# Two expert phases of a one-core macaron kernel: a wait inside the scatters, another order for the first statistics, and tables built in five parts

## What is computed

```python
x = x + 0.5 * ffn(layernorm(x)); x = x + mamba(layernorm(x)); x = x + 0.5 * ffn(layernorm(x))
def ffn(x):                       # x: 2048 tokens of 512
    logits = x @ router_w.T       # 8 experts, the 2 best of each token
    scores, top_idx = top_k(logits, 2)
    y_e = (silu(x @ wg[e]) * (x @ wu[e])) @ wd[e]          # e: 8 experts, inner width 256
    shared = silu(x @ sg_w + sg_b) * (x @ su_w + su_b) @ sd_w + sd_b
    return sum_over_best(scores * y_e) + shared
```

## Time and profile before

| | |
|---|---|
| median of 3 runs | 2316.42 us (2307.47 to 2318.51) |
| profiled execution | 2313.75 us, span 2312.0 us, mean granted TensorE clock 0.967 |
| PE, DVE, ACT, POOL busy | 93%, 64%, 62%, 60% of the span |
| `ffn1`, `ffn2` in the span | 0 to some 360 us, 1953.7 to 2312 us |

### The profile page before, as it was taken

One profiled execution on the slowest core, in us unless ns is written; L12 is line 12 of the kernel. 1 busy time (PEld: TensorE's weight loads), 2 busy tenths in 40 slices (PEclk: granted clock), 3 DMA queues, 4 the chain that ended last, 5 costly groups with the idle time before them and its releaser, 6 DMA issues. The chain is left out here.

```text
span 2312.0 us, 42896 instructions
## 1 busy us (share of the span) xinstructions
PE 2156.3 (93%) x11718; PEld 1744.5 (75%) x11718; DVE 1474.8 (64%) x2947; ACT 1432.8 (62%) x2960; POOL 1376.3 (60%) x1242
## 2 busy tenths in 40 slices
PE   5899996899999999999988999999999997789996
PEld 3687774688888888888767888888888885577775
DVE  6532247577777677777887777777777778732225
ACT  5133323777787778787658787778777774423331
POOL 2886351476666667666517666667666663586622
PEclk8999997899999999999999999999999998899998
DMA  9665361334334333433214434334433431555545
GB/s 345 243 189 175 115 174 42 101 111 108 106 84 119 106 101 99 119 97 93 65 49 127 110 86 126 98 98 105 113 102 88 117 85 35 186 188 164 160 142 164
DMA packets 204904, 285.32 MB, mean 123 GB/s; under 512 B 16288, under 2 KB 148458, under 8 KB 204816
## 3 DMA queue, kind: packets, MB, share of 16 engines
q1 hardware_dynamic: 185936, 219.18, 33.1%
q0 software_dynamic: 18880, 65.02, 9.3%
HBM read 225.43 MB, written 58.72 MB: 123 GB/s over the span
## 5 line engine op out<-in xcount | busy, mean ns | idle before, releaser
L2057 PE MATMUL mamba_p_proj<-mamba_xt_lo,mamba_in_hi 128*128 128x512 f32 x1056 | 456.9, 433 | 1.6 <-DVE mamba_bc L1708 1.1
L1708 DVE SCALAR_TENSOR_TENSOR mamba_xs<-mamba_p_proj,mamba_taps,mamba_xs 128x511 f32<-128x511 f32 (+2 forms) x384 | 285.8, 744 | 258.9 <-ACT mamba_xs L1455 250.0
L2059 PE MATMUL mamba_p_proj<-mamba_xt_hi,mamba_in_lo 128*128 128x512 f32 x1056 | 416.2, 394 | 0.0
L2058 PE MATMUL mamba_p_proj<-mamba_xt_hi,mamba_in_hi 128*128 128x512 f32 x1056 | 414.0, 392 | 0.0
L1328 POOL TENSOR_TENSOR mamba_xend<-mamba_xdt,mamba_to_end_g 128x512 f32<-128x512 f32 x128 | 134.0, 1047 | 340.0 <-DVE mamba_xdt L1768 282.8
L1334 POOL TENSOR_TENSOR mamba_mix<-mamba_mix,mamba_scores 128x512 f32<-128x512 f32 x256 | 326.5, 1297 | 14.2 <-ACT mamba_mix L1521 14.2
L1517 ACT ACTIVATE mamba_mix<-mamba_cum_l,mamba_cum_g 128x128 f32<-128x128 f32 x1024 | 324.7, 388 | 8.7 <-DMA mamba_cum_l<-mamba_cum_rows 3.8
L664 DVE TENSOR_TENSOR ffn_h<-ffn_p_gu,ffn_sil 128x256 f32<-128x256 f32 x110 | 46.8, 426 | 317.9 <-ACT ffn_sil L546 303.9
L546 ACT ACTIVATE ffn_sil<-ffn_p_gu 128x256 f32<-128x256 f32 x110 | 42.3, 385 | 319.4 <-PE ffn_p_gu L913 237.5
L2059 PEld LDWEIGHTS mamba_p_proj<-mamba_xt_hi,mamba_in_lo 128*128 128x128 f32 x1056 | 199.6, 189 | 46.5
L2057 PEld LDWEIGHTS mamba_p_proj<-mamba_xt_lo,mamba_in_hi 128*128 128x128 f32 x1056 | 200.7, 190 | 40.7 <-DVE mamba_bc L1708 2.0
(11 more groups left out here) (344 smaller groups left out, 5095.0 us busy)
## 6 DMA issues: line engine op xcount, KB each, us to landing
mamba_cum_l<-mamba_cum_rows SPq DMA_DIRECT2D x128, 512.0 KB, 5.3
mamba_rise<-mamba_exp_rows SPq DMA_DIRECT2D x256, 128.0 KB, 3.4
ffn_xs<-slots_in SPq DMA_DIRECT2D x78, 256.0 KB, 2.7
slots_out<-ffn_y SPq DMA_DIRECT2D x78, 256.0 KB
mamba_raw_x<-in_t SPq DMA_DIRECT2D x34, 512.0 KB, 5.5
mamba_raw_z<-in_t SPq DMA_DIRECT2D x32, 512.0 KB, 6.4
mamba_raw_out<-out_t SPq DMA_DIRECT2D x32, 512.0 KB, 4.7
slots_out<-ffn_xs SPq DMA_DIRECT2D x1, 9984.0 KB
```

Source lines behind the costliest of these rows:

```text
L1708: dve.scalar_tensor_tensor(dst[:, i:BLK], p_proj[:, ct, 0:BLK - i], tap[:, 0, j:j + 1], dst[:, i:BLK], ALU.mult, ALU.add).then_inc(s_conv, 1)
L2057: pe.matmul(bank, in_hi[:, piece, kk, :], xt_lo[:, kk, c], start=(kk == 0), stop=False)
L2058: pe.matmul(bank, in_hi[:, piece, kk, :], xt_hi[:, kk, c], start=False, stop=False)
L2059: last = pe.matmul(bank, in_lo[:, piece, kk, :], xt_hi[:, kk, c], start=False, stop=(kk == KT - 1))
```

## The change

1. `scatter`: before the scatters of the third, fifth and seventh tile of a half POOL waits until all earlier ones have landed. That is three waits in a half, six in a phase.
2. `ffn1` alone: SP issues all four loads of x first, then the router's and the biases'. POOL issues the three first weight loads after its four memsets and no longer before them.
3. Statistics: `ffn1` takes blocks 0 and 1 ahead of the tiles. Then in both phases the statistics of a block come tile by tile, two blocks ahead, between the `low_l` of DVE (`ahead`, `stat_tile`, `moments_tile`, `variance`), with `scale` at a block's first tile. `roots` of ACT moves to fit.
4. Tables: `turns` becomes `turns_first` (7 instructions and the copy that lets SP start its fills), `turns_second` (5), `turns_third` (9), `order_pairs` becomes two parts; they lie after ticks 1, 2, 3, 4 and 5. Before, `turns` lay after tick 2 and `order_pairs` after tick 3.

```diff
+        def ahead(t):
+            first, count = ((0, 2), (2, 1), (3, 1), (4, 0))[t % TPB]
+            first += (t // TPB + 2) * TPB
+            return range(first, first + count) if first < T else range(0)
...
             if hidden is not None:
-                load_x(0)
+                for b in range(NB):
+                    load_x(b)
             sp.dma_start(router[:, :, :], ...).then_inc(s_router, 16)
...
-                for b in range(1, NB):
-                    load_x(b)
                 sp.wait_ge(s_zero, 1)
...
             def scatter(half):
                 pool.wait_ge(s_route, half + 1)
                 for t in range(half * HALF, (half + 1) * HALF):
+                    if t % HALF != 0 and t % 2 == 0:
+                        pool.wait_ge(s_scat, 2 * t * 16)
                     for k in range(2):
                         pool.indirect_dma_start(
...
-            load_gate(0); load_up(0); load_out(0)
+            if hidden is None: load_gate(0); load_up(0); load_out(0)
             (four memsets)
+            if hidden is not None: load_gate(0); load_up(0); load_out(0)
...
         act:
                 if t + AHEAD < T:
-                    if (t + AHEAD) % TPB == 0 and not known:
-                        roots((t + AHEAD) // TPB)
                     rows(t + AHEAD)
+                if t == 0 and not known:
+                    roots(1)
                 high_l(t)
-                if known and t % TPB == TPB - 1 and t // TPB + known < NB:
-                    roots(t // TPB + known)
+                if t % TPB == TPB - 1 and t // TPB + 2 < NB:
+                    roots(t // TPB + 2)
...
         dve:
+            def stat_tile(t):
+                if hidden is not None and t % TPB == 0:
+                    dve.wait_ge(s_x[t // TPB], 16)
+                if t > known * TPB:
+                    dve.wait_ge(s_stat, 2 * (t - known * TPB))
+                dve.bn_stats(stat[:, t % TPB, :], x[:, t, :]).then_inc(s_stat, 1)
+            def moments_tile(t):
+                dve.wait_ge(s_stat, 2 * (t - known * TPB) + 1)
+                dve.bn_aggr(moments[:, t, :], stat[:, t % TPB, :]).then_inc(s_stat, 1)
...
                 scale(0)
+                stats(1)
             for t in range(T):
-                b = t // TPB + max(known, 1)
-                if known and t % TPB == 0 and known < b <= NB:
-                    scale(b - 1)
-                if t % TPB == 0 and b < NB:
-                    stats(b)
+                if t % TPB == 0 and known <= t // TPB + 1 < NB:
+                    scale(t // TPB + 1)
                 low_l(t)
-                if not known and t % TPB == 0 and b < NB:
-                    scale(b)
+                for u in ahead(t):
+                    stat_tile(u)
+                    moments_tile(u)
+                if t % TPB == TPB - 2 and t + 2 * TPB < T:
+                    variance(t // TPB + 2)
...
             tick(1)
+            turns_first()
             tick(2)
-            turns()
+            turns_second()
             tick(3)
+            turns_third()
+            tick(4)
             order_pairs()
-            for g in range(4, JOBS):
+            tick(5)
+            share_pairs()
+            for g in range(6, JOBS):
```

More of the change, by code:

```diff
@@ L426, in _ @@
             build_identity(pool, ident[:, :], s_const, 0)
-            load_gate(0)
-            load_up(0)
-            load_out(0)
+            if hidden is None:
+                load_gate(0)
+                load_up(0)
+                load_out(0)
             pool.memset(one[:, :], 1.0).then_inc(s_const, 1)
@@ L433, in _ @@
             pool.memset(bias_out[:, :].bitcast(F32), 0.0).then_inc(s_const, 1)
+            if hidden is not None:
+                load_gate(0)
+                load_up(0)
+                load_out(0)
             pool.wait_ge(s_const, 6)
@@ L619, in stats, with variance @@
                     dve.bn_aggr(moments[:, b * TPB + t, :], stat[:, t, :]).then_inc(s_stat, 1)
-                dve.wait_ge(s_stat, n + 2 * TPB)
+                variance(b)
+            def stat_tile(t):
[7 more added lines that the diff above has]
+                dve.bn_aggr(moments[:, t, :], stat[:, t % TPB, :]).then_inc(s_stat, 1)
+            def variance(b):
+                dve.wait_ge(s_stat, (b - known + 1) * 2 * TPB)
                 s = slice(b * TPB, (b + 1) * TPB)
@@ L753, in places, with turns_first @@
                 dve.tensor_copy(slot[:, :, ts], slot_f[:, :, ts]).then_inc(s_route, 1)
-            def turns():
+            def turns_first():
                 step = link(dve, s_rank, 42)
@@ L764, in turns, with turns_second @@
                 step(dve.tensor_scalar(gap[:, :], count[:, :], -1.0, float(ROOM), ALU.mult, ALU.add))
+            def turns_second():
+                step = link(dve, s_rank, 48)
                 step(dve.tensor_tensor(passed[:, :, :], end[0:1, :].unsqueeze(1).broadcast_to([1, TILES, E]),
@@ L771, in turns, with turns_third @@
                 step(dve.tensor_tensor(wrap[:, 0, :], wrap[:, 0, :], tile_no[:, :], ALU.add))
+            def turns_third():
+                step = link(dve, s_rank, 53)
                 step(dve.tensor_scalar(table[:, 3, :], wrap[:, 0, :], float(P), None, ALU.mult))
@@ L792, in order_pairs, with share_pairs @@
                 step(dve.tensor_tensor(ordered[:, 1, :], slot_f[:, 0, :], slot_f[:, 1, :], ALU.max))
+            def share_pairs():
+                step = link(dve, s_rank, 70)
                 step(dve.tensor_scalar(weight[:, :, :], best[:, :, :], 0.5, None, ALU.mult))
```

## The result

The changed kernel takes 2336.23 us (median of 5 runs, 2332.81 to 2337.76), the kernel before 2315.7 us beside it. The ratio is 1.0091, with a 95% interval of 1.0073 to 1.0109: slower by 0.9%. The forecast was 2337 us. The loss is 20.5 us between the medians, 22.7 in the forecast's sum. The profiled execution has a span of 2335.4 us against 2312.0.

What follows compares the result with a forecast made beforehand. Scatters were taken to be last at `columns(9)`, PE the bound after it. 9.2 (`ffn1`) + 8.0 (`ffn2`) + 5.5 (clock) = 22.7 us on 2313.75 gave 2336.5, stated as 2337 us; range 2306 to 2354, own case alone 2322 to 2351.

Steps and rivals of the forecast that it cites:

- The chain: GpSimd's scatters up to `columns(9)`: nothing covers a wait's landing, as the next scatter is what the chain needs.
- The rival by which ACT's stalls were the larger evil: Scatters of both phases: a wait costs 0.5 us net, `columns(9)` comes 4.0 and 5.2 us sooner, 2304.5 us; chance 0.12.
- scatters and PE meet in `ffn1`: At `columns(9)` of `ffn1` before the change: both arrive almost together, scatters last, PE idle only 0.72 us.
- The start: DVE's work before the first scatters: `ffn1` gains 7 us (4 to 10), `ffn2` 1 us (0 to 2).
- with statistics two blocks ahead: Start of `ffn1`: DVE should idle about as little as in `ffn2`, 12.3 - 5.4 = 6.9 us less.
- The waits: GpSimd's scatters: 2.7 us for each of six waits a phase, 16.2 us together (13.8 to 21.6).
- my lower bound: Net price of one scatter wait: 2.3 us, from SP going on 2.66 us after the last scatter's issue.
- the first wait would cost a few us more: Scatters: applies if the zeroing still runs when they start; the later zeroing was costed at nothing.
- an estimate of 2.6 us: Landing of a 256 KB transfer: about 2.0 us fixed plus bytes over 436 GB/s; six waits 13.8 us net.
- The sum at `columns(9)`: First routed tile on PE: starts 9.2 us later in `ffn1` and 8.0 us later in `ffn2`.
- The tables: `turns` in five parts: PE's 1.16 us idle goes, but PE waits for the scatters later, so worth nothing.
- The clock: PE after its idle before `columns(9)`: lower clock for 6 us, 2.8 us a phase, +5.5 us in both.

Runs made afterwards that it cites:

- a_nowait: Changed kernel without the six waits in each phase's scatters, all else kept: 2321.68 us, ratio 1.0013 to the kernel before.
- b_wait: Kernel before with only the six waits in each phase's scatters added: 2336.54 us, ratio 1.0077.
- m_before: Kernel before, unchanged, run again for its profile: group median 2314.81 us, profiled execution 2320.81 us.
- d_lag_block: Changed kernel with scatter waits one group further back, and `ffn2`'s statistics again by block: 2306.9 us, ratio 0.9950 to the kernel before.
- k_router: Changed kernel, waits included, with SP's load order of before (one x block, router, biases, other x blocks): 2313.76 us, ratio 1.0097 to the kernel before.
- p_tables: Kernel before with only the tables in five parts between ticks: 2325.96 us, ratio 1.0051.
- o_start_block: Changed kernel without scatter waits and with `ffn2`'s statistics by block as before: 2313.16 us, ratio 1.0002 to the kernel before.
- n_after: Changed kernel, run again unaltered in the third group: 2338.78 us, ratio 1.0109 to the kernel before.
- c_lag: Changed kernel with scatter waits one group further back, at most eight scatters outstanding: 2309.06 us, ratio 0.9958 to the kernel before.

## Why the prediction was right

**The chain.** The step on which all rests was that, with the waits, the scatters are last at `columns(9)` and that nothing covers a landing. PE's idle of 30.20 and 23.54 us there shows it, a_nowait and b_wait from both sides. The rival by which ACT's stalls were the larger evil predicted 2304.5 us; the stalls before `columns(9)` did vanish, and the time rose. What the prediction took from one profile is less firm: that scatters and PE meet in `ffn1`. In m_before the last scatter starts 0.5 us sooner than in the first profile and `columns(9)` 5.9 us later, so PE was last there by some 6 us. From that profile the same sum would have given `ffn1` about 6 us less.

**The start.** 7 us taken for `ffn1`, 6.5 measured at the first scatter, with DVE's idle at 5.6 us where 5 to 6 was named. For `ffn2` a gain of 1 us was taken and 2.4 us were lost. That sign was wrong: the step "with statistics two blocks ahead" overlooked that a block's statistics had filled DVE's wait for the first transposes, and d_lag_block gives the 2.4 us back.

**The waits.** 16.2 us a phase were taken, 13.8 to 21.6 the bounds. `ffn1` paid 19.0, `ffn2` 13.45, just under the lower bound. Where nothing else ran a wait was 2.0 us of idle (1.7 net), under my lower bound of 2.3; where fills or weights ran beside it 2.9 to 3.7 (5.2 and 5.3 once a phase in b_wait), near the gathers' 3.1 and 3.9; and the first of `ffn1` 6.54. That one was named ("the first wait would cost a few us more") and then costed at nothing. k_router shows that it is 4.5 us: its first wait is 2.02 us. The Trainium skill's fit (DMA: Bandwidth & Descriptors, Anatomy of one DMA), from which I had an estimate of 2.6 us for such a transfer, lies between the 2.0 us measured from the end of the last issue and the 3.0 from its start.

**The sum at `columns(9)`.** +9.2 forecast and +12.8 measured, +8.0 forecast and +8.1 measured. The first is short by the waits (2.8 us) and the start (0.5). The second agrees by luck: the start came out 3.4 us worse than taken and the waits 2.8 cheaper. From the end of the last scatter to `columns(9)` it was 5.2 us, as taken.

**The tables.** They were put at nothing, because PE waits for the scatters at a later tick. Under the waits no run isolates them. Alone on the kernel before, where PE didn't wait for the scatters, they cost 11 us (p_tables), and a_nowait and o_start_block, without waits, lie 3 us above and 0.5 above before by their ratios where a gain was expected. So "nothing" isn't shown for this term, and p_tables speaks against it outside the changed kernel.

**The clock.** 5.5 us were taken, about half is there. PE's timeline after its idle in `ffn1`:

```profile
117.64 0.63 PE L991 MATMUL ffn_p_dn<-ffn_out_hi,ffn_ht_hi 128*128 128x512 f32 x1
118.07 0.63 PE L992 MATMUL ffn_p_dn<-ffn_out_hi,ffn_ht_lo 128*128 128x512 f32 x1
118.50 0.47 PE L990 MATMUL ffn_p_dn<-ffn_out_lo,ffn_ht_hi 128*128 128x512 f32 x1
118.81 0.39 PE L991 MATMUL ffn_p_dn<-ffn_out_hi,ffn_ht_hi 128*128 128x512 f32 x1
```

Products stood 0.43 us apart until 118.50, 2.6 us after `columns(9)` began, where the earlier trace rows gave 6. The granted clock was 0.50 (the lower level, 1.2 GHz) from 115 to 118 us, 0.67 in the next and 1.00 (2.4 GHz) from 119 on, and in `ffn2` 0.50 from 2068 to 2071 and 0.96 in the next microsecond. From `columns(9)` to SP's ninth load `ffn1` lost 1.3 us on before and `ffn2` 1.5, together 2.8.

**The total.** By phases the forecast was +12.0 and +10.7. The profiles give +14.5 for `ffn1` (mamba starts at 378.28, 363.76 before), +5.9 for `ffn2` and +3.0 for the mamba stage, which no part of the change touches and which was 1588.5 us long in n_after and 1592.9 here. The mechanism and the size of a phase's loss are shown. That the total agrees to 1 us is luck: `ffn1` lost 2.5 us more than forecast, `ffn2` 4.8 less, and 3.0 are in a stage that had no term.

## What to carry over

Before a wait is put between transfers that form a chain, ask what would be late without it: a landing cost 2 to 4 us here, 5 to 6.5 at worst, and is paid in full when its engine issues the next link, however long the stalls that it cures elsewhere. Where the number outstanding must be bounded, wait for the group before the last one: that form was 12.6 us faster than no wait in the first group (c_lag), though alone on the kernel before it cost 3.6 us in the second. Work that looks early can be filling another engine's latency; a move that helps one phase has to be read again in the phase that starts from another state.

## What the runs showed of the hardware

- ACT's unnamed stalls beside free-running scatters come and go between groups of runs of the same code: 17 to 31 us a phase where the kernel before took 2315 to 2318 us, none where it took 2290 us. With at most four scatters outstanding (the changed kernel twice, b_wait) there were none before `columns(9)` either. Chip number 9 had a group of either kind, so whether the chip or its state decides isn't known, nor what stalls ACT.
- The same stalls stand beside the gathers at a phase's end, in every profile where the kernel before took 2315 to 2318 us, and that stretch is 8 to 11 us longer there than where it took 2290 us.
- SP's issue of a small load behind four of 1 MB took 4.08 us, and the next 4.87, against 0.50 and 0.41 behind one (k_router). Queueing a large load ahead holds back the engine that issues, not only the data: the zeroing that waits for `s_zero` came 12 us later, where I had worked out 8.
- A group of four 256 KB scatters with nothing beside it has landed 2.0 us after the issue of the last one ended: 22 of the 36 waits in the changed kernel, b_wait and k_router idled 2.00 to 2.03 us. The other 14 idled 2.8 to 6.5 us. Counted from the start of the last issue, 0.97 us earlier, this is 3.0 us.
